# Writing out the loop over four images on every engine of a four-layer convolution kernel

## The reference

```
x = x + L0(gn(x))   # 3x3 convolution on values quantised to int8, scale from the maximum over ALL four images
x = x + L1(gn(x))   # real part of a 2-D Fourier transform, 32x32 modes mixed over channels, transformed back
x = x + L2(gn(x))   # 1x1 convolution, pooled to 5x5 filters, applied depthwise to its own input
x = x + L3(gn(x))   # maxima over unfolded 3x3 patches -> 1x1 convolution, norm, relu -> weights of the patches
```

## Time and profile before

| | us |
|---|---|
| median of 3 runs | 3399.25 (3398.79 to 3400.56) |
| the profiled execution, whole | 3398.91 |
| its span, from the first to the last instruction | 3397.2 |
| PE busy | 2683.0 (79%) |
| DVE busy | 2677.4 (79%) |
| POOL busy | 1822.7 (54%) |
| ACT busy | 1817.6 (54%) |
| mean granted TensorE clock | 0.921 of full |

### The profile page before, as it was taken

The page is one execution under the profiler, slowest core; times in us unless marked ns, Lnnn a source line. Parts: engine busy times, 40 slices in busy tenths (PEclk is TensorE's granted clock), DMA queues, the critical chain, the costliest instruction groups (busy, mean ns, idle before and its releaser), DMA issues.

```text
span 3397.2 us, 49036 instructions
## 1 busy us (share of the span) xinstructions
PE 2683.0 (79%) x12701; PEld 2086.3 (61%) x12701; DVE 2677.4 (79%) x3571; ACT 1817.6 (54%) x2351; POOL 1822.7 (54%) x1296
## 2 busy tenths in 40 slices
PE   0085698699989479599989469879998847959998
PEld 0044576577757358487764458657774645848776
DVE  8985887688875898588878588768888588858887
ACT  7652655566643455456645165556664445545664
POOL 2013172599940436199990317259994044619998
PEclk9997899899999789799999779989999978979999
DMA  6722002888850200778880200288884020078884
GB/s 254 251 60 87 7 0 69 237 195 195 191 146 13 81 1 0 224 182 195 194 221 16 93 1 0 80 235 192 195 191 139 21 73 0 0 225 191 192 195 118
DMA packets 117493, 421.31 MB, mean 124 GB/s; under 512 B 16821, under 2 KB 30949, under 8 KB 106634
## 3 DMA queue, kind: packets, MB, share of 16 engines
q1 hardware_dynamic: 96438, 376.17, 42.9%
q10 hardware_dynamic: 19332, 38.99, 3.3%
q0 software_dynamic: 1616, 4.90, 0.5%
HBM read 340.44 MB, written 75.26 MB: 122 GB/s over the span
## 4 chain that ended last, share of the span: by engine, by line
PE 62%; DVE 14%; issue 14%; DMA 3%; POOL 3%; ACT 2%; DVEq 1%; ACTq 1%; SPq 0%; POOLq 0%
PE psum L549 26%; PE psum L516 16%; PE psum L425 8%; PE psum L451 3%; PE psum L489 3%; POOL work L880 2%; PE psum L527 2%; PE psum L437 2%; DVE work L1077 2%; DVE small L920 2%; DVE small L921 1%; DMA workr<-mx_dram 1%; DVE work L1091 1%; DVE work L1282 1%; DVE work L1287 1%
## 5 line engine op out<-in xcount | busy, mean ns | idle before, releaser
L880 POOL TENSOR_TENSOR work<-work 128x512 f32<-128x512 f32 x960 | 1278.3, 1336 | 470.6 <-DVE work L1291 363.4
L549 PE MATMUL psum<-workr,w 128*128 128x512 f32 (+1 forms) x5760 | 1367.6, 398 | 125.4 <-DMA workr<-mx_dram 110.1
L549 PEld LDWEIGHTS psum<-workr,w 128*128 128x128 f32 (+1 forms) x5760 | 1090.5, 190 | 401.7 <-issue 111.0
L1282 DVE SCALAR_TENSOR_TENSOR work<-psum,work 128x512 f32<-128x512 f32 x1152 | 741.9, 681 | 71.8 <-PE psum L549 54.5
L516 PE MATMUL psum<-workr 128*128 128x512 f32 x2304 | 553.2, 403 | 21.6 <-DVE workr L1179 21.6
L854 POOL TENSOR_TENSOR work<-img 128x520 f32 (+1 forms) x256 | 387.8, 1547 | 288.2 <-DVE workr L1151 258.9
L516 PEld LDWEIGHTS psum<-workr 128*128 128x128 f32 x2304 | 441.3, 192 | 135.0 <-issue 24.9
L844 POOL TENSOR_TENSOR work<-work 128x1024 f32<-128x1024 f32 x40 | 112.5, 2843 | 500.1 <-DVE work L1066 495.9
L726 ACT CAST workr<-psum 128x650 fp32r<-128x650 f32 x128 | 90.2, 704 | 446.1 <-DVE psum L1258 239.2
L425 PE MATMUL psum<-work,taps 128*128 x1152 | 259.0, 388 | 55.1 <-DVE work L1024 55.1
L1255 DVE TENSOR_TENSOR psum<-psum,work 128x650 f32<-128x650 f32 x128 | 107.9, 843 | 236.6 <-ACT psum L719 236.5
(11 more groups left out here) (186 smaller groups left out, 3666.3 us busy)
## 6 DMA issues: line engine op xcount, KB each, us to landing
work<-gn_dram SPq DMA_DIRECT2D x256, 585.0 KB, 11.5
work<-gn_dram SPq DMA_DIRECT2D x256, 146.2 KB, 3.7
work<-gn_dram SPq DMA_DIRECT2D x128, 292.5 KB, 4.7
work<-in_x SPq DMA_DIRECT2D x16, 2048.0 KB, 7.1
img<-in_x SPq DMA_DIRECT2D x32, 1024.0 KB, 11.7
work<-in_mixw SPq DMA_DIRECT2D x64, 512.0 KB, 4.0
out_x<-work ACTq DMA_DIRECT2D x120, 256.0 KB, 5.9
gn_dram<-img SPq DMA_DIRECT2D x24, 1040.0 KB, 21.7
```

What stands on the lines that cost most here:

```text
L549: mm = T.matmul(bank(m % 6), w5[wt][0:kr, P * n:P * n + P], ft[0:kr], start=(i == 0), stop=(i == 4))
L880: G.tensor_tensor(acc_t[v], acc_t[v], pd_t[(9 * v + n) % 6], ALU.add).then_inc(s_acc, 1)
L1282: V.scalar_tensor_tensor(out=tile4(pd_t[m % 6]), in0=tile4(psum[:, m % 6, :]), scalar=0.0, in1=rv[:, q, y0:y0 + RT, x0:x0 + WO], op0=ALU.m ...
```

## The change

Eight loops are hit: the prepass loop on SP, ACT and DVE is a Python loop now, and so is the main loop on all five engines. The image number b becomes a constant in each of four copies of the body. The loops inside an image stay hardware loops. Nothing else is touched: the same operations, in the same order, with the same waits for the same values. The whole diff:

```diff
-            with sp.Fori(0, B) as b:        # L301, prepass
+            for b in range(B):
-            with sp.Fori(0, B) as b:        # L312
+            for b in range(B):
-            with pe.Fori(0, B) as b:        # L414
+            for b in range(B):
-            with act.Fori(0, B) as b:       # L563, prepass
+            for b in range(B):
-            with act.Fori(0, B) as b:       # L577
+            for b in range(B):
-            with pool.Fori(0, B) as b:      # L837
+            for b in range(B):
-            with v.Fori(0, B) as b:         # L917, prepass
+            for b in range(B):
-            with v.Fori(0, B) as b:         # L982
+            for b in range(B):
```

## The result

| | before | after |
|---|---|---|
| median, us | 3399.78 (3398.79 to 3401.38, 6 runs) | 3379.64 (3375.73 to 3381.03, 6 runs) |
| ratio | 1 | 0.9938, 95% interval 0.9926 to 0.9951 |
| profiled execution, whole, us | 3398.91 | 3380.86 |
| its span, us | 3397.2 | 3379.0 |

The change takes 20 us, 0.6%; the forecast was 3384.0 in a range of 3377 to 3394. The two profiled executions lie 18.2 us apart by their spans.

What follows compares the result with a forecast made beforehand. PE carries 62% of the chain of waits, but between images everything hangs on DVE's stall behind its jump back. 13.9 + 0.8 + 0.3 + 0.8 - 0.9 = 14.9 us off 3398.91 gives 3384.0, range 3377 to 3394.

Steps and rivals of the forecast that it cites:

- The jumps, 13.9 us: DVE's three backward jumps of the main loop between images: stalls of 4.58, 4.74 and 4.60 us go in full.
- the loop's own instructions, 0.8: Register and branch instructions of DVE's main loop L982: 0.26 us at each of three turns go.
- Rival (b): At image borders: the stall comes wherever new code is late, not from the jump; about 3397 us, 8%.
- rival (a): A loop inside an image lies badly and reloads code every turn; 22 us per tile-loop copy, 3406 us, 5%.
- The signs: Chain of waits after: L1015 within 0.3 us of the last L1282, PE's first L425 about 5.6 us after it.
- The sign of being wrong: An "issue" piece of over 3 us anywhere else in the changed kernel's chain of waits would show the prediction wrong.
- POOL's remaining sums touch nothing that the next image's start needs.: At image borders: POOL's last sums were taken not to delay the next image, so nothing was deducted.
- The first load, 0.3: At the prepass' start, SP's loop and address instructions before the first load: 0.3 of 0.39 us go.
- Waits inside an image, 0.8 in 0 to 6: Waits become constants on DVE; 0.2 us an image in the third normalisation goes, 0.8 in all, at most 6.
- The prepass, nothing: Turns of the prepass loop on SP, ACT and DVE are hidden under DVE's 32 reductions of 4.4 us: 0.
- The clock, 0.9 lost in 2.7 either way: TensorE's clock after PE's idle time between images: 0.3 us lost a turn, within 2.7 us gained or lost in all.
- The price of a branch: Counter-rule at the main loop's turns: about 108 ns per compare-and-branch, so 0.3 us for three turns, about 3397.5 us.

Runs made afterwards that it cites:

- Experiment 1: Kernel before with only DVE's main loop (L982) written out; all other loops kept: 3381.99 us, ratio 0.9946.
- experiment 2: Kernel before with the main loops of SP, PE, ACT and POOL written out; DVE's and the prepass loops kept: 3400.67 us, ratio 1.0002.
- experiment 9: Kernel before with the prepass written out and every engine's main loop going over two images a turn, one jump back left: 3386.44 us, ratio 0.9963.
- experiment 5: Changed kernel with POOL's sums of each image's last tile cut to 8 of 512 columns, its last turn written out: 3373.38 us, ratio 0.9921.
- the repeat: The changed kernel itself, unaltered, run and profiled again: 3380.87 us, ratio 0.9946.
- experiment 6: Kernel before with only the three prepass loops (SP, ACT, DVE) written out, all main loops kept: 3394.1 us, ratio 0.9982.
- experiment 8: Changed kernel with the three prepass loops kept, so only the five main loops are written out: 3376.79 us, ratio 0.9931.
- experiment 7: Two kernels: the kernel before again, unchanged, 3398.79 us; and the kernel before with only DVE's prepass loop (L917) written out, 3395.31 us.
- experiments 3: Changed kernel put inside a hardware loop of one turn, its register added to the image number (folded into a constant): 3378.95 us, ratio 0.994.
- experiment 10: Changed kernel with next image's coefficients set before the tile loop and two chunks scaled early: 3373.86 us; the same with prepass loops kept: 3372.5 us.

## Why the prediction was right, point by point

**The jumps, 13.9 us, and the loop's own instructions, 0.8.** Right in size and in kind: 14.6 us between the profiles at the three borders. Experiment 1 has it with DVE's loop alone, experiment 2 keeps it with DVE's loop kept, and experiment 9 puts it at the one border with a jump. Rival (b), that new code is late wherever it comes, has fallen: four copies of new code come without a stall of this size. No idle time of DVE or PE over 2.5 us is put down to "issue" in the trace of the kernel after, so rival (a) did not come either. The signs had to be read from the timelines, for the chain of waits of the kernel after reaches back only to 2995 us. The sign of being wrong was badly set: "issue" pieces of over 3 us stand elsewhere in the chain before as well (3.91 us at 606.42).

**"POOL's remaining sums touch nothing that the next image's start needs."** This step failed. They share no data with it, but they slow DVE's roundings from 1.23 us to between 1.8 and 2.3 us, and 3.6 us of the gain went back (experiment 5), for which the sum had no term. The prediction looked for who waits for POOL and not for who works beside it; DVE's stall had kept the two apart. PE's first matmul came 6.8 us after the last product, not 5.6.

**The first load, 0.3.** 0.5 us were gained up to the first L1015 (0.7 in the repeat). That the prepass' loops gave it isn't shown: with them alone written out it is 0.0 (experiment 6), with them kept 0.3 (experiment 8), and the two profiles of the kernel before differ by 0.2 (171.41 and 171.19).

**Waits inside an image, 0.8 in 0 to 6.** The row chosen for it was real, but its cause was not. Its 0.2 us were no register instruction on the path but an instruction that comes late at a fixed place of the code (experiment 7). The main term was elsewhere: "in inner loops each wait still needs its register j, so their register instructions stay; PE covers them in any case". They stay, but those with two registers became cheaper (132 to 63 ns), and PE does not cover them in full: it waits 2 to 5 us less for DVE in the tile loop (experiment 9). With the 1.8 us of the two late instructions this is 4 to 7 us, where 0.8 was taken and 6 was the upper end. That the tile loop's whole 5.4 us come from the registers isn't shown: experiment 6 has 4.9 of them with every register kept.

**The prepass, nothing.** As time of the prepass itself it was nothing. As a change of where the main loop's code lies it was worth 4 to 6 us ahead of the old main loop (experiments 6 and 7), and nothing ahead of the new one (experiment 8). The forecast had no term for the place of the code but rival (a), which wanted a load of code at every turn of a loop. That did not come.

**The clock, 0.9 lost in 2.7 either way.** At the three borders of the profile it was a gain (0.86 against 0.77, 1.6 us in layer 0 over all images). In the repeat the three borders show 0.71, 0.73 and 0.87, and layer 0 took 275.9 us against 275.7. So the clock went either way, as the range allowed, and over several runs it is about nothing.

**The price of a branch.** The rule of 108 ns for a compare-and-branch (the Trainium skill, "Advanced Engine Details and Errata", Control Flow Timing) would have given 3397.5. This case does not agree: the branch itself took 0.06 us in experiment 9's chain, about half the page's figure, and 4.32 us of "issue" stand behind it, which the figure does not hold.

The sum, then: 14.6 + 0.5 + 5.4 + 2.2 + 1.6 - 3.6 - 2.8 and 0.3 of small entries are the 18.2 us between the profiles. The forecast of 14.9 us was right in its main term. That it came within 3.3 us of the 18.2 is in part luck: 6.4 us were lost that it had at nothing, and 9.2 us were gained (tile loop, L1082 to L516, layer 0) where it had 0.8 gained and 0.9 lost.

**What stays open.** Why L437 to L1082 takes 397.1 and 398.2 us in the two profiles of the full change, 394.3 and 395.3 in those of before, and 395.9 and 395.8 in experiments 3 and 8. L1073 is part of it: 1638 ns on the mean after, 1537 before and 1588 in its repeat. Where the 2 to 4 us of the prepass' effect beyond the 1.8 come from. Which of PE's, ACT's and POOL's register terms is the one felt, and how the tile loop's 5.4 us divide between them and the place of the code; each kernel that removes them also moves code.

## What to carry to other kernels

A backward jump over a long body cost 4.3 to 4.7 us on DVE here, with a load of code in each stall, and it counts only on the engine that the next turn waits for: look in the chain of waits for a short branch followed by "issue", and write out that engine's loop first. When a stall goes, look not only at who was waiting but at what the stall kept apart from it in time. And before giving a meaning to 0.1 or 0.2%, try the same kernel with its code moved: here a change that touches nothing later moved the time by 4 to 6 us.

## What the runs showed of the hardware

- Behind DVE's jump back over the whole body the next instruction came 4.3 to 4.7 us later, and a packet of code on q14 lay in each of 16 such stalls.
- Beside GpSimd's f32 sums (L880, 128x512) VectorE's TENSOR_SCALAR operations (L1022, L1024, 128x2048) mostly take 1.6 to 2.3 us instead of 1.23; with the sums gone they take 1.23 at the same moment. The sums take 2.12 us instead of 1.27 there, and the two engines' operations end by turns, 1.09 and 1.12 us behind one another. One rounding beside a sum took 1.29 us only (experiment 10).
- At fixed places of straight code the next instruction of DVE comes 0.18 to 0.27 us late, in each image, and a packet of code starts 0.57 to 0.97 us behind it. On a chain of 0.19 us steps it is felt; with the code moved it isn't there.
- Four written-out copies needed fewer packets of code (46 and 38) than the loop (61 and 46).
- DVE's register instruction at L1310 takes 132 ns with the image's register and the tile's, 63 ns with the tile's alone; at L1279 107 and 46 ns.
